# First attention of a six-layer decoder: copies of two heads in four move to VectorE, and waits at the start of three attentions are set anew

## The reference

```
q = x @ W_q;  k = x @ W_k;  v = x @ W_v
latent_kv = (k + v) @ W_down_kv
k_rec, v_rec = latent_kv @ W_up_k, latent_kv @ W_up_v      # 16 heads of 16
scores = q_h k_rec_h^T / sqrt(256) * decay                  # 512 x 512 a head
attn = softmax(scores);  out = attn @ v_rec;  return out @ W_o
```

## Time and profile before

| | us |
|---|---|
| median of three runs | 3807.51 |
| lowest and highest | 3801.92, 3808.04 |
| the profiled execution | 3794.37 |
| its span | 3792.5 |
| TensorE busy (share of the span) | 3267.4 (86%) |
| VectorE busy | 2024.4 (53%) |
| ScalarE busy | 1912.7 (50%) |
| GpSimd busy | 972.8 (26%) |

### The profile page before, as it was taken

One profiled execution on the slowest core, in us unless ns is written; L12 is line 12 of the kernel. 1 busy time (PEld: TensorE's weight loads), 2 busy tenths in 40 slices (PEclk: granted clock), 3 DMA queues, 4 the chain that ended last, 5 costly groups with the idle time before them and its releaser, 6 DMA issues. The chain is left out here.

```text
span 3792.5 us, 75673 instructions
## 1 busy us (share of the span) xinstructions
PE 3267.4 (86%) x26784; PEld 2538.5 (67%) x26784; DVE 2024.4 (53%) x6791; ACT 1912.7 (50%) x4678; POOL 972.8 (26%) x790
## 2 busy tenths in 40 slices
PE   7888888879889589999899887999999966999990
PEld 4666566558778466666666565777777755999980
DVE  5777777766667455555554553466666642000007
ACT  5888788744532165556555553655555531222210
POOL 0000000026300376777677640000111121000006
PEclk8999999988899799999999998999999987999995
DMA  5111011100100222222122211000000025555544
GB/s 186 54 53 60 35 52 52 62 5 1 65 1 1 65 53 51 58 55 57 46 57 51 53 45 51 13 13 18 24 23 25 24 97 172 183 185 183 181 146 130
DMA packets 128784, 254.79 MB, mean 67 GB/s; under 512 B 24928, under 2 KB 67360, under 8 KB 123552
## 3 DMA queue, kind: packets, MB, share of 16 engines
q1 hardware_dynamic: 117520, 198.55, 17.5%
q0 software_dynamic: 10896, 51.39, 3.6%
HBM read 159.03 MB, written 57.28 MB: 57 GB/s over the span
## 5 line engine op out<-in xcount | busy, mean ns | idle before, releaser
L987 PE MATMUL a_T<-ident,a_t 128*128 128x128 f32 x3328 | 500.8, 284 | 91.0 <-ACT a_pT L1155 63.8
L987 PEld LDWEIGHTS a_T<-ident,a_t 128*128 128x128 f32 x3328 | 376.0, 144 | 285.8 <-issue 250.4
L1155 ACT ACTIVATE a_pT<-a_T 128x512 f32<-128x512 f32 (+3 forms) x768 | 368.9, 512 | 225.2 <-PE a_T L987 225.1
L1396 DVE CUSTOM_DVE_ANT_0 a_t<-a_A,a_decay 128x512 f32<-128x512 f32 x512 | 323.0, 687 | 101.8 <-PE a_A L952 101.6
L1168 ACT ACTIVATE a_t<-a_t,a_neg 128x512 f32<-128x512 f32 x512 | 362.6, 716 | 5.8 <-DVE a_neg L1407 4.6
L1401 DVE CUSTOM_DVE_ANT_0 a_t<-a_A,a_table 128x384 f32<-128x384 f32 (+3 forms) x512 | 221.1, 487 | 174.2 <-PE a_A L964 173.5
L1227 POOL TENSOR_TENSOR a_rsin<-a_rawswapped,a_sin 128x512 f32<-128x512 f32 x128 | 170.7, 1333 | 520.1 <-DMA a_rawswapped<-a_raw 431.8
L2446 DVE COPY experts_y<-experts_Y 128x256 f32<-128x256 f32 x72 | 30.6, 425 | 497.5 <-PE experts_Y L2387 497.5
L2428 ACT ACTIVATE experts_hT<-experts_H 128x512 f32<-128x512 f32 x144 | 86.0, 597 | 415.0 <-PE experts_H L2401 415.0
L1168 ACT ACTIVATE a_t<-a_t,a_mx 128x384 f32<-128x384 f32 (+3 forms) x512 | 280.0, 551 | 0.0
L2401 PEld LDWEIGHTS experts_H<-experts_xgT,experts_w 128*128 128x128 f32 x2304 | 270.9, 193 | 8.4 <-issue 3.8
(11 more groups left out here) (334 smaller groups left out, 6738.6 us busy)
## 6 DMA issues: line engine op xcount, KB each, us to landing
experts_w<-in_f_w_dram SPq DMA_DIRECT2D x72, 1024.0 KB, 5.0
moe_sent<-a_zeros POOLq DMA_DIRECT2D x33, 1024.0 KB, 8.4
a_rawswapped<-a_raw SPq DMA_DIRECT2D x512, 64.0 KB, 2.0
a_invrep<-a_inv_dram SPq DMA_DIRECT2D x64, 256.0 KB, 4.0
experts_xg<-moe_sent SPq DMA_DIRECT2D x72, 128.0 KB, 2.0
moe_results<-experts_y SPq DMA_DIRECT2D x72, 128.0 KB, 1.9
x_invrep<-x_inv_dram SPq DMA_DIRECT2D x32, 256.0 KB, 3.9
ex_w<-in_f_w_dram SPq DMA_DIRECT2D x8, 1024.0 KB, 12.9
```

The source lines that it names most:

```text
L987: mm = pe.transpose(bank[:, kt, :], t_of(u, j, kt * P, (kt + 1) * P), sh.ident[:])
L1155: nc.scalar.activation(to, of, ACT.Copy).then_inc(t_empty, 1)
L1396: nc.vector.tensor_tensor_reduce(t_of(s, j, 0, n), A[seg.bank(name)][:, 0:n], table[:, at:at + n], 1.0, LOWEST, ALU.mult, ALU.max, mx[:, s ...
```

## The change

In a0, heads 1 and 3 are now copied by VectorE and heads 0 and 2 by ScalarE, so that each T bank has one reader. VectorE's copies go through a new function `turn_head`; head 1's stands at j = 2 of a step, behind the reciprocal and the tasks at j = 0 and 1 and ahead of a task at 2; head 3's stays where it was. The counts of `t_empty` and `t_copied` follow. In all three attentions VectorE posts its credits before anything else, and in a1 and x1 the waits of TensorE and ScalarE for `ready` move from the start of their programs to the second task.

```diff
-            pe.wait_ge(ready, N_READY)
+            if a0:
+                pe.wait_ge(ready, N_READY)
...
                 free = [(t_empty, job + 1)] if x1 else \
+                    [(t_copied if j % 2 else t_empty, 2 * ug + j // 2 + 1)] if a0 else \
                     [(t_copied, ug + 1)] if j == 1 else [(t_empty, ug * 3 + (2, 0, 3, 4)[j])]
...
-                    if not x1:
+                    if a0:
+                        pe.wait_ge(t_empty, (b * U + u_v + 1) * 2 + 1)
+                        pe.wait_ge(t_copied, (b * U + u_v + 1) * 2 + 1)
+                    elif a1:
                         pe.wait_ge(t_empty, (b * U + u_v + 1) * 3 + 2)
                         pe.wait_ge(t_copied, b * U + u_v + 2)
...
                     if work == START[1]:
                         pe.wait_ge(weights, LOADED)
+                        pe.wait_ge(ready, N_READY)
...
-            act.sem_inc(t_empty, 2)
-            act.wait_ge(ready, N_READY)
+            act.sem_inc(t_empty, 1 if a0 else 2)
+            if a0:
+                act.wait_ge(ready, N_READY)
...
-                    if do_t and j < (T_UNIT if x1 else 3):
+                    if do_t and j in ((0, 2) if a0 else range(T_UNIT if x1 else 3)):
...
                 for work in START:
+                    if work == START[1] and not a0:
+                        act.wait_ge(ready, N_READY)
...
         def _(dve):
+            dve.sem_inc(a_dve, A_BANKS)
+            dve.sem_inc(o_empty, 2)
+            if not x1:
+                dve.sem_inc(t_copied, 1)
...
                 dve.wait_ge(weights, LOADED)
                 dve.wait_ge(ready, N_READY)
-            dve.sem_inc(a_dve, A_BANKS)
-            dve.sem_inc(o_empty, 2)
-            if not x1:
-                dve.sem_inc(t_copied, 1)
...
+            def turn_head(ug, j):
+                u = ug % U
+                wait_apart(dve, (ready, N_READY), (pv, ug + 1), (t_full, ug * T_UNIT + (j + 1 + T_CREDIT)))
+                kts, bank = keys(u) // P, T[(u * T_UNIT + j) % 2]
+                nc.vector.tensor_copy(p_tile(u, j, 0, kts), bank[:, 0:kts, :] if kts > 1 else bank[:, 0, :])\
+                    .then_inc(t_copied, 1)
...
                         advance(norm[0], 2)
+                    if a0 and j == 2 and s < U and (own if s >= LAG_T else prev):
+                        turn_head(b * U + s - LAG_T, 1)
                     for head, work in found:
...
-                u_t = s - LAG_T
-                if not x1 and s < U and (own if u_t >= 0 else prev):
-                    u = u_t % U
-                    wait_apart(dve, (ready, N_READY), (pv, b * U + (u_t + 1)),
-                               (t_full, (b * U + u_t) * T_UNIT + (4 + T_CREDIT)))
-                    kts, bank = keys(u) // P, T[(u * T_UNIT + 3) % 2]
-                    nc.vector.tensor_copy(p_tile(u, 3, 0, kts), bank[:, 0:kts, :] if kts > 1 else bank[:, 0, :])\
-                        .then_inc(t_copied, 1)
+                if not x1 and s < U and (own if s >= LAG_T else prev):
+                    turn_head(b * U + s - LAG_T, 3)
```

## The result

The changed kernel takes 4040.56 us (median of four runs, 4033.53 to 4044.83), the kernel before 3804.72 (four runs beside it): ratio 1.0606, 95% interval 1.0585 to 1.0626. It is slower by 236 us by the medians and by 231 by the ratio. 4030 was forecast, with a range of 3950 to 4115. The profiled execution after took 4033.53 us (span 4031.7).

The account below looks back on a forecast made before the run. No engine was full; loops through several engines bound the first attention. 180 + 45 - 3 = +222 us on the profiled 3794.4 gave 4016, plus 13.1 to the median: 4030, range 3950 to 4115.

Parts of the forecast that it names:

- The loop: First attention: head 3, value product and next scores queue behind VectorE's late copy of head 1; +180 us.
- The clock: First attention: TensorE's new stops drop its clock in four steps of ten, 0.9 us each; +45 us.
- the stop: TensorE's wait before head 3 for VectorE's copy of head 1, 1.9 us in nearly every step.
- no fall: Rival: first attention's steps lengthen but TensorE's clock never drops; 3985 us, chance 0.25.
- a fall in nearly every step: Rival: TensorE's clock drops in nearly every step of the first attention; 4115 us, chance 0.14.
- The starts: Two later attentions: first transposes run while weights land, about 1.5 us left of each 2.6 gain; -3 us.
- both banks are drained at once: Rival, first attention: ScalarE and VectorE copy side by side, saving 0.53 us a step; 3739 us, chance 0.04.
- VectorE's work alone: Rival, first attention: only VectorE's added copy counts, 125 x 0.68 = 85 us; 3890 us, chance 0.08.

Follow-up runs that it names:

- part 3: Kernel before with only VectorE's credits posted first and the two later attentions' waits for `ready` moved, copies unchanged: 3805.3 us, ratio 0.9976.
- the idle multiply: Kernel before plus one VectorE multiply a step into an unread spare tile, where the changed kernel copies head 1: 3807.2 us, ratio 0.9999.

## Why the prediction was right, step by step

**The loop (forecast +180).** The shortest step of each place among batches 2 to 7, which leaves the clock's falls out as far as it can, sums to 92.8 us a batch before and 115.9 after: +23.1, where the forecast had 23.0. By kind, forecast and measured:

| kind (places in a batch) | forecast | measured |
|---|---|---|
| plain, value projection (3) | 1.69 | 1.71, 1.79, 1.65 |
| query projection (4) | 2.04 | 2.08, 2.08, 2.17, 2.08 |
| key projection (4) | 1.76; 1.45 with the row turn | 1.72, 1.78, 1.83, 1.33 |
| turn of the sums (2) | 0.9 | 0.88, 0.87 |
| row addition (2) | 0.75 | 0.70, 0.71 |
| transposes of x (1) | -0.3 | -0.30 |

The rule behind them (the next scores start 2.36 us after VectorE reaches copy 1) holds: 607.45 to 609.83 is 2.38. Each link has an experiment: the place (copy earlier, 199 us back), what is queued behind the wait (value product first, 157 back), and not the work (VectorE busier, 0 within 7 us).

**The clock (forecast +45).** The stage grew by 235.4, so 55 are left beside the loop's 180; refilling the stop gave 45 back, and 57 with its own cost counted. The term was some 10 us small. In batches 2 to 7, 50 steps of 96 are over 0.25 us longer than the shortest of their place, 7 were before, and 49 of the 50 hold time at the lower clock; in the whole stage that is 196 us after and 48 before. The share was 0.45 (50 less 7, of 96) where I took 0.4. Each costs a net 0.95 where I took 0.9. The two rivals on either side, no fall and a fall in nearly every step, are both out by this count. That the falls would come was reasoned from the rows; the share of four in ten rested on two or three of them, and that it came so near is in part luck. Two smaller parts were off: the stop of a plain step is 1.65 us and not 1.9, since head 2 is done 2.8 us after the scores and not 2.6, and in the query step shown above value product and scores lose 0.91 us together where 0.5 was estimated.

**The starts (forecast -3).** From the first load to the first copy of a query projection's result, a1's start went from 16.61 to 14.44 us and x1's from 17.08 to 14.62: 2.2 and 2.5 less, where I took 1.5 each. The first projections start 2.8 and 2.6 us sooner after the first load, as forecast, so the stretch at half clock took 0.6 and 0.15 of the gain where I took 1.1. Alone, part 3 measured 9 us, between 2 and 16, which holds the 4.7 of the two traces.

**The sum.** 180 + 55 - 5 = 230, against a ratio that makes 223 to 238 us of the 3804.72. The forecast's 222 is at the lower edge, and the 10 us lack in the clock's term.

**What the forecast got for another reason.** It set out from the profiled execution and added 13.1 us up to the median. That this execution was short in its last section by some 20 us (98.3 against 119.5), I did not see; the way through the difference to the median made it good. A comparison of the two profiled executions alone, 239.2 us, would have laid 17.8 of that section on the change. Layers behind the first attention were 11.9 us shorter after, up to the first gather, 4.7 of it at the starts; the other 7 are no more than single executions differ there (with the idle multiply, which touches none of those layers, that part took 2901.7 us; 2913.3 before, 2901.4 after).

**Two readers of PSUM side by side.** In the plain step above ScalarE copies head 0 at 605.23 and VectorE head 1 at 607.45: the order of VectorE's queue kept the two copies apart. So the rival in which both banks are drained at once (3739) is out, as is that of VectorE's work alone (3890). The Trainium skill, PSUM — Partial Sum Buffer, Specifications (TRN2), says that ScalarE and VectorE read PSUM side by side at full rate when they are in different banks. The trace agrees as far as it goes: ScalarE's copy of head 0 (605.23, 0.60 us) runs beside VectorE's scores (0.69 us each, from 604.72 on). The rule did not decide here.

## What to carry to other kernels

An instruction moved to a less busy engine takes that engine's queue with it: look where in the order it will stand, when the engine comes to that place, and who is queued behind its result. The sum along that loop, one step from mark to mark, gave each kind of step within 0.14 us here, while busy shares (VectorE at 73% of the stage) said that there was room. When a wait appears in every step, price TensorE's clock as a second term (55 of the 231 us here), and compare a stretch of the two traces, not whole executions.

## What the runs showed of the hardware beyond that

- Twelve more transposes in each step, and nothing else, took the granted clock of 60 to 740 us from 0.91 to 0.99 of full speed.
- The last section takes 98 us or 113 to 120: VectorE's short instructions there stand now and then 1 to 4 us for what the profile calls "remote" or "issue". Only the first profile of the kernel before has the 98. What decides between the two was not tried.
- 0.66 us more of VectorE's work in each of 128 steps cost nothing measurable (0.9999, 0.9981 to 1.0018), though it stood between the reciprocal and a copy on which the value product of the next step depends.
